# Cross-attention on one core: the low weights' last 64 rows as row halves beside the scores, for V as for K

## What is computed

```python
h = _layernorm(x, gamma, beta)                       # x: 8 x 256 x 256
Q = (h @ Wq).reshape(B, NQ, N_HEADS, HEAD_DIM)       # Wq: 256 x 1024
K = (context @ Wk).reshape(B, NC, N_HEADS, HEAD_DIM) # context: 8 x 256 x 192
V = (context @ Wv).reshape(B, NC, N_HEADS, HEAD_DIM)
attn = jnp.einsum('bihd,bjhd->bhij', Q, K)
attn = jax.nn.softmax(attn, axis=-1) * scale
vals = jnp.einsum('bhij,bjhd->bihd', attn, V).reshape(B, NQ, INNER)
out = x + vals @ Wo + bo
```

## Time and profile before

| What | Value |
|---|---|
| median of three runs | 364.79 us |
| the profiled execution, time of its run | 364.5 us |
| its span, first to last instruction | 362.6 us |
| what lies around the span | 1.9 us |
| granted TensorE clock over the span | 0.999 of full speed |
| busy: PE, DVE, ACT, POOL | 97%, 67%, 70%, 45% |
| share of the chain that ended last: PE | 92% |

### The profile page before, as it was taken

How to read it: one execution, slowest core, us unless ns; L and a number is a source line. 1 busy time by engine, 2 the same in 40 slices (tenths; PEclk the granted TensorE clock), 3 DMA queues, 4 the chain that set the end, 5 groups by cost and what they waited for, 6 DMA issues and landing times.

```text
span 362.6 us, 8915 instructions
## 1 busy us (share of the span) xinstructions
PE 353.0 (97%) x3116; PEld 305.8 (84%) x3116; DVE 242.9 (67%) x534; ACT 252.1 (70%) x762; POOL 164.5 (45%) x321
## 2 busy tenths in 40 slices
PE   5999999999999999999999999999999999999986
PEld 5779888888888888988888988888988888988865
DVE  5887566866568666686667675686565866566654
ACT  4898876766677766777766776766677766677762
POOL 5677884335444262444532464323744325344321
PEclk9999999999999999999999999999999999999999
DMA  6930010200002000020000100020000000000000
GB/s 191 272 118 3 1 52 2 82 0 3 2 0 82 0 0 0 0 80 0 1 0 29 51 0 0 0 78 1 0 0 0 29 2 0 2 2 31 3 0 31
DMA packets 10743, 10.39 MB, mean 29 GB/s; under 512 B 960, under 2 KB 10176, under 8 KB 10720
## 3 DMA queue, kind: packets, MB, share of 16 engines
q1 hardware_dynamic: 10192, 9.64, 8.6%
q10 hardware_dynamic: 416, 0.33, 0.3%
q0 software_dynamic: 112, 0.13, 0.2%
HBM read 8.00 MB, written 2.10 MB: 28 GB/s over the span
## 4 chain that ended last, share of the span: by engine, by line
PE 92%; ACT 3%; DVE 3%; DMA 1%; issue 0%; POOL 0%; DVEq 0%
PE mix_ps L710 16%; PE st_ps L805 15%; PE st_ps L688 13%; PE o_ps L777 12%; PE w_ps L752 12%; PE w_ps L730 12%; PE w_ps L823 10%; ACT prob L405 2%; DMA x_in<-in_x_dram 1%; PE w_ps L671 1%; PE w_ps L663 1%; ACT qk_hi L415 0%; DVE w_lo L480 0%; DVE neg_max L563 0%; DVE qk_lo L576 0%
## 5 line engine op out<-in xcount | busy, mean ns | idle before, releaser
L316 POOL TENSOR_SCALAR prob<-prob,inv 128x256 f32<-128x256 f32 x256 | 120.1, 485 | 158.0 <-DVE inv L570 157.6
L405 ACT ACTIVATE prob<-st_ps,neg_max 128x256 f32<-128x256 f32 x256 | 118.0, 473 | 27.0 <-DVE neg_max L563 27.0
L563 DVE TENSOR_REDUCE neg_max<-st_ps 128x2 f32<-128x512 f32 x128 | 82.5, 683 | 35.2 <-PE st_ps L688 34.9
L458 ACT ACTIVATE prob_t<-st_ps 128x512 f32<-128x512 f32 x64 | 38.4, 600 | 44.2 <-PE st_ps L805 44.2
L638 DVE COPY prob_t<-st_ps 128x512 f32<-128x512 f32 x64 | 44.1, 691 | 28.6 <-PE st_ps L805 25.2
L710 PE MATMUL mix_ps<-prob_t,v_sb 128*64 128x256 f32 x504 | 61.5, 385 | 0.1
L805 PE MATMUL st_ps<-ident,prob 128*128 128x128 f32 x512 | 61.1, 272 | 0.0
L805 PEld LDWEIGHTS st_ps<-ident,prob 128*128 128x128 f32 x512 | 56.7, 141 | 0.1
L576 DVE TENSOR_TENSOR qk_lo<-w_ps,qk_hi 128x512 fp32r<-128x512 f32 x62 | 42.8, 690 | 20.6 <-ACT qk_hi L415 20.6
L405 ACT ACTIVATION_READ_ACCUMULATOR prob<-st_ps,neg_max 128x1 f32 x256 | 52.7, 206 | 0.0
L710 PEld LDWEIGHTS mix_ps<-prob_t,v_sb 128*64 128x64 f32 x504 | 33.4, 136 | 17.9 <-issue 0.3
(11 more groups left out here) (121 smaller groups left out, 589.1 us busy)
## 6 DMA issues: line engine op xcount, KB each, us to landing
x_in<-in_x_dram SPq DMA_DIRECT2D x8, 256.0 KB, 3.1
out_dram<-y_sb SPq DMA_DIRECT2D x7, 256.0 KB, 2.2
c_in<-in_ctx_dram SPq DMA_DIRECT2D x7, 192.0 KB, 2.9
w_raw<-in_L_xattn_Wq_dram SPq DMA_DIRECT2D x8, 128.0 KB, 3.3
w_raw<-in_L_xattn_Wo_dram SPq DMA_DIRECT2D x4, 256.0 KB, 3.5
w_raw<-in_L_xattn_Wk_dram SPq DMA_DIRECT2D x4, 128.0 KB, 4.0
w_raw<-in_L_xattn_Wk_dram SPq DMA_DIRECT2D x8, 64.0 KB, 3.6
w_raw<-in_L_xattn_Wv_dram SPq DMA_DIRECT2D x2, 256.0 KB, 3.5
```

The costliest lines, as they stand in the source:

```text
L316: last = nc.gpsimd.tensor_scalar(prob[:, e, r, :], prob[:, e, r, :], inv[:, e, r:r + 1], SCALE, ALU.mult, ALU.mult)
L405: last = nc.scalar.activation(prob[:, e, r, :], st_ps[e][:, r * ROWS:(r + 1) * ROWS], ACT.Exp, bias=neg_max[:, e, r:r + 1], accum_out=sums ...
L458: nc.scalar.activation(prob_t[:, e, :, :].rearrange("p a b -> p (a b)"), st_ps[e][:, :], ACT.Copy)\
L563: nc.vector.tensor_reduce(neg_max[:, e, :], st_ps[e][:, :].rearrange("p (r j) -> p r j", r=RT), AX, ALU.max, negate=True).then_inc(max_rea ...
```

## The change

- **K.** For steps 1 to 30, each pair's product with the last low rows is left out of `keys`. A new `keys_rest(u)`, between `scores(u)` and `mix(u - 1)`, does both pairs at once: the first pair on rows 0 to 63 of the array and the second on rows 64 to 127, 64 rows each, the high part of the context alone. It opens the banks `w0_ps` and `w1_ps`, and so waits for `v_ready`.
- **V.** From the third V on, the 512 columns are halved over `w0_ps` and `w1_ps`: four products of 256 columns for each half at the end of a step, and the last low rows as two 64-row products (`values_rest`) at the start of the next step, ahead of the scores. ACT copies V out in two pieces.
- **A second copy** of the high part's last 64 rows, `c_rest`, on partitions 0 to 63: one more ACT piece in `context_hi`.
- **Order of the turns.** As V's second half takes `w1_ps`, `turn_c` and `turn_x` stand between `output(u - 1)` and `turn(u)`, each behind a wait for both `qk_lo` of the step. `context_hi` and `context_lo` move into the context step, ahead of the copies of `prob_t`; `norm` moves to the end of the context step, behind these copies; `hidden` moves into the x step; `statistics` move one step ahead. V's second half waits for `context_lo` or for the first half of `hidden` where such a turn was made.
- **PE's program** has no loop any more.

```diff
+    V_HALF = GROUP * P // 2
+        c_rest = sb("c_rest", [HALF, 2, ROWS], fp32r)
-        LOAD, STATS, TURN_C, NORM, SPLIT_C, SPLIT_H, PUT = -5, -4, -4, -3, -3, -2, PER_SEQ + 1
+        LOAD, STATS, TURN_C, TURN_X, SPLIT_H, PUT = -5, -5, -4, -3, -2, PER_SEQ + 1
...
             def context_hi(b, ps):
                 nc.scalar.activation(c_t[:, b % 2, 0, :], ps[:, 0:ROWS], ACT.Copy)
+                nc.scalar.activation(c_rest[:, b % 2, :], ps[HALF:P, ROWS:2 * ROWS], ACT.Copy)
...
                 if 2 <= u < STEPS:
-                    values_out(u, w0_ps)
+                    act.wait_ge(v_made, u + 1 + turns(8))
+                    for k, ps in enumerate((w0_ps, w1_ps)):
+                        last = nc.scalar.activation(
+                            v_sb[:, u // RT % 2, u % RT, k * V_HALF:(k + 1) * V_HALF],
+                            ps[:, 0:V_HALF], ACT.Copy)
+                    last.then_inc(v_ready, 1)
...
+                b = of_seq(u, TURN_C, 2)
+                if b is not None:
+                    act.wait_ge(c_turned, b + 1 + turns(2))
+                    context_hi(b, context_bank(b))
+                b = of_seq(u, TURN_X, 1)
+                if b is not None:
+                    act.wait_ge(h_lo_ready, DT * b + turns(4))
+                    act.wait_ge(x_turned, b + 1 + turns(2))
+                    hidden(b, w1_ps)
...
+            def keys_rest(u):
+                b, p = divmod(BATCH * (u + 1), PAIRS)
+                pe.wait_ge(v_ready, RT if u == 1 else u + 1)
+                pe.wait_ge(qk_lo_ready, BATCH * (u + 1))
...
+                high = (c_rest[:, b % 2, :], c_t[HALF:P, b % 2, 1, :])
+                for a in range(BATCH):
+                    own = slice(a * HALF, (a + 1) * HALF)
+                    nc.tensor.matmul(qk_banks(u)[a][:, 0:ROWS],
+                                     w_lo[own, K0 + 1, (p + a) * P:(p + a + 1) * P], high[a],
+                                     start=True, stop=False, skip_group_check=True)
...
+                for a in range(2):
+                    pe.wait_ge(qk_lo_ready, BATCH * n + a + 1)
+                    seq = of_seq(n - 1, TURN_C, 2)
+                    if a == 1 and seq is not None:
+                        pe.wait_ge(c_lo_ready, seq + 1)
+                    seq = of_seq(n - 1, TURN_X, 1)
+                    if a == 1 and seq is not None:
+                        pe.wait_ge(h_full_ready, DT * seq + 1)
+                    first = half * PIECE + a * V_HALF
+                    for m, (w, i, k) in enumerate(passes[:-1]):
...
+                        nc.tensor.matmul((w0_ps, w1_ps)[a][:, 0:V_HALF], c_t[:, b % 2, k, rows],
+                                         w[:, i, first:first + V_HALF],
+                                         start=m == 0, stop=False, skip_group_check=True)
+            def values_rest(n):
...
+                high = (c_rest[:, b % 2, rows], c_t[HALF:P, b % 2, 1, rows])
+                for a in range(2):
+                    own = slice(a * HALF, (a + 1) * HALF)
+                    first = half * PIECE + a * V_HALF
+                    last = nc.tensor.matmul((w0_ps, w1_ps)[a][:, 0:V_HALF], high[a],
+                                            w_lo[own, V0 + 1, first:first + V_HALF],
+                                            start=False, stop=True, skip_group_check=True)
+                last.then_inc(v_made, 1)
...
+            def step(u):
+                if 2 <= u < STEPS:
+                    values_rest(u)
                 if 0 <= u < STEPS:
-                    scores(u, turns)
+                    scores(u)
+                if 1 <= u < STEPS - 1:
+                    keys_rest(u)
...
+                b = of_seq(u, TURN_C, 2)
+                if b is not None:
+                    pe.wait_ge(c_loaded[b % 2], 16 * (b // 2 + 1))
+                    pe.wait_ge(qk_lo_ready, BATCH * u + HEADS)
+                    turn_c(b, context_bank(b))
+                b = of_seq(u, TURN_X, 1)
+                if b is not None:
+                    pe.wait_ge(x_norm_ready, b + 1)
+                    pe.wait_ge(qk_lo_ready, BATCH * u + HEADS)
+                    turn_x((w1_ps, w1_ps), ROWS)
                 if 0 <= u < STEPS:
-                    turn(u, turns)
+                    turn(u)
                 if 1 <= u < STEPS - 1:
-                    values(u + 1, turns)
...
-            walk(pe, step, 2)
+            for u in range(-1, LAST):
+                step(u)
```

More of the change, by code:

```diff
@@ L308, in step @@
                     weight_lo(14)
-                b = of_seq(u, NORM, 1)
+                b = 1 if u == 1 else of_seq(u, TURN_C, 2)
                 if b is not None:
@@ L388, in step @@
                 if 2 <= u < STEPS:
-                    values_out(u, w0_ps)
[L390 to L399, removed]
+                    act.wait_ge(v_made, u + 1 + turns(8))
[4 more added lines that the diff above has]
+                    last.then_inc(v_ready, 1)
+                if u == 1:
+                    act.wait_ge(c_turned, 2)
+                    context_hi(1, context_bank(1))
                 def probabilities(e):
@@ L583, in step @@
                 maximum(1)
-                b = of_seq(u, SPLIT_C, 1)
-                if b is not None:
-                    context_lo(b, context_bank(b), turns)
+                if u == 1:
+                    context_lo(1, context_bank(1), turns)
                 maximum(2)
@@ L627, in step @@
                     weight_lo(16)
-                if b is not None and b >= 2:
-                    dve.wait_ge(x_turned, b + turns(2))
-                    norm(b, turns)
+                b = of_seq(u, TURN_C, 2)
+                if b is not None:
+                    context_lo(b, context_bank(b), turns)
                 if 0 <= u < STEPS:
@@ L641, in step @@
                             weight_lo(13)
+                b = of_seq(u, TURN_C, 2)
+                if b is not None:
+                    dve.wait_ge(x_turned, b + turns(2))
+                    norm(b, turns)
                 b = of_seq(u, STATS, 2)
@@ L716, in mix, with keys @@
                         last.then_inc(mixed, 1)
-            def keys(t, a, turns, parts=(0, 1)):
+            def keys(t, a, parts=(0, 1)):
                 b, p = divmod(t, PAIRS)
@@ L756, in queries, with output @@
                 last.then_inc(projected, 1)
-            def output(w, turns):
+            def output(w):
                 b, s = divmod(w, PER_SEQ)
@@ L798, in last_output, with turn @@
                             last.then_inc(o_added, 1)
-            def turn(u, turns):
+            def turn(u):
                 for e in range(HEADS):
-                    pe.wait_ge(scaled, HEADS * u + e + 1 + turns(32))
+                    pe.wait_ge(scaled, HEADS * u + e + 1)
                     for r in range(RT):
@@ new lines, in values_rest @@
+            def values_rest(n):
+                g, j = divmod(n, RT)
+                b, half = divmod(g, 2)
+                rows = slice(j * P, (j + 1) * P)
+                high = (c_rest[:, b % 2, rows], c_t[HALF:P, b % 2, 1, rows])
[5 more added lines that the diff above has]
+                                            start=False, stop=True, skip_group_check=True)
@@ L836, in _ @@
             for a in range(BATCH):
-                keys(a, a, lambda n: 0)
+                keys(a, a)
             for a in range(BATCH):
-                queries(a, a, lambda n: 0)
+                queries(a, a)
             for a in range(BATCH):
-                keys(BATCH + a, a, lambda n: 0, parts=(0,))
-            def step(u, turns):
+                keys(BATCH + a, a, parts=(0,))
+            def step(u):
+                if 2 <= u < STEPS:
+                    values_rest(u)
                 if 0 <= u < STEPS:
-                    scores(u, turns)
+                    scores(u)
+                if 1 <= u < STEPS - 1:
+                    keys_rest(u)
                 if 1 <= u <= STEPS:
-                    mix(u - 1, turns)
+                    mix(u - 1)
                 for a in range(BATCH):
@@ L850, in step @@
                     if 0 <= u and t < BATCH * STEPS:
[L851 to L866, removed]
+                        keys(t, a, parts=(1,) if u == 0 else (0, 1))
+                        queries(t, a)
                 if 1 <= u < STEPS:
-                    output(u - 1, turns)
+                    output(u - 1)
                 if u == STEPS:
```

89 lines of the change are left out of this document (49 added, 40 removed).

## The result

The changed kernel takes **370.79 us** (median of five runs, 370.58 to 371.05), the kernel before 364.80 us beside it. The ratio is 1.0166, with a 95% interval from 1.0152 to 1.0180: 1.7% slower, 6.0 us. Forecast were 370.9 us, slower with a chance of 0.86.

The account below looks back on a forecast made before the run. PE was taken as the bound in every step. Saving -5.7, start +0.4, context steps +4.0, x steps +6.6 and step 1 +0.8 sum to +6.1 on 364.5, so 370.6; the median 0.3 above, 370.9 us; range 365.4 to 373.0.

Parts of the forecast that it names:

- The saving: PE, steps 1 to 30: K 0.12 and V 0.07 less, together 0.19 a step, -5.7 us.
- the third rival: The halves don't run side by side: two pairs a step cost 0.12 more each, +7.2, 378.1 us; chance 0.03.
- the first rival: Faster, the waits don't show: saving stays, only the start's 0.4 is paid, -5.3, 359.5 us; chance 0.07.
- The start: Before the first scores: a third piece in `context_hi` delays PE, bounds 0 and 0.4, taken as +0.4 us.
- The wait ahead of the turns: PE between `output` and the turn waits for `qk_lo`: 0.31 plus 0.16 restart, 0.47 us lost.
- the restart: PE going on after a wait costs more, read from step 31: 0.05 + 0.11 = 0.16 us.
- V's second half, and the late maximum: Context step: PE loses 0.19 waiting at V's second half; DVE starts the x step's maximum 0.78 us late.
- The x steps: ACT catches up 0.15 of 0.78, so PE waits 1.10 ahead of `turn_x`; six steps, +6.6 us.
- Step 1: `norm` stands ahead of its second `qk_lo`: a wait between 0.47 and 1.10, taken as +0.8 us.
- The three waits: PE's waits in six context steps (+4.0), six x steps (+6.6) and step 1 (+0.8 us).
- Nothing carries over: All 13 turns from step 1 cost 0.47, but x steps' DVE and V's second half aren't late: 365.6 us; chance 0.12.
- The program's packets: PE's written-out program needs some 13 more instruction packets; rival if PE waits for each: +12, 382.9 us; chance 0.02.

Follow-up runs that it names:

- the kernel with the low part behind the copies: Changed kernel with the turned context and x put in `mix_ps`, and `context_lo` placed after DVE's two copies of `prob_t`: 359.43 us, ratio 0.9854 to the kernel before.
- The edit of `norm`: Against the changed kernel, `norm` of the third and later sequences goes back into the x step, between the second inverse and `mix_lo`: 367.66 us.

## Why the prediction was right

**The saving.** Forecast were 0.12 for K and 0.07 for V in a step; undone one at a time, plain steps grow by 0.12 (K, in the changed kernel) and 0.07 (V, in the kernel with the low part behind the copies). The halves do run side by side. K's pair in a plain step of the changed kernel:

```profile
224.64 0.28 PE L766 MATMUL w_ps<-c_rest,w_lo 64*128 64x256 f32 x1
224.65 0.28 PE L766 MATMUL w_ps<-c_t,w_lo 64*128 64x256 f32 x1
```

That settles the third rival. With the waits taken away, the kernel comes to the first rival's time: 359.43 against 359.5. Its condition, `qk_lo` before `output`, did not hold; a bank that needs no `qk_lo` does the same.

**The start.** +0.4 forecast. The first keys wait for the context's low part until 8.32, 7.95 in the earlier trace rows, and the first scores start at 12.65 instead of 12.26: +0.39.

```profile
8.32 0.42 PEld L748 LDWEIGHTS w_ps<-c_t,w_hi 128*128 128x128 f32 x3 [0.64 <-DVE c_t L523]
```

**The wait ahead of the turns.** 0.47 forecast, 0.47 measured in the context step. It comes apart as worked out: `qk_lo` ends at 196.32 + 0.69 = 197.01, and `output` would have gone on at 196.57 + 0.12 = 196.69, so 0.32 (forecast 0.31); PE starts 0.15 after `qk_lo` (forecast 0.16 for the restart). The restart's size was right, but not how it falls: the prediction read it from step 31 as 0.05 ahead of the first product and 0.11 behind it.

**V's second half, and the late maximum.** Here two terms were off, and they offset each other. The low part ends at 199.46 + 0.43 = 199.89, 2.27 after the turn's start (forecast 2.26), and PE goes on at 200.03, 0.19 lost as forecast. But the products behind the restart run slower too, another 0.07, which the step left out. That makes the context step 11.64 instead of the 11.5 forecast. It also moves the next scores back, so that the maximum, 202.49 - 197.62 = 4.87 after the turn (forecast 4.90), is 0.69 late and not 0.78.

By the sentence of the Trainium skill that the prediction draws on (VectorE: DVE Perf Modes, section The DRAIN you can't avoid) that start would have been 0.21 later. The same paragraph goes on that a next operation that is not held starts earlier. The rows fit that: 0.74 for the two pieces of `norm`, and 1.88 for three maxima where a single one takes 0.69.

**The x steps.** The mis-sized term: 1.10 forecast, 0.96 measured. From the lateness of 0.69, `qk_lo` keeps 0.50 (its end is 209.14 - 201.06 = 8.08 after the scores, 230.96 - 223.38 = 7.58 in the plain step), so ACT and DVE caught up 0.19 instead of 0.15. 0.47 + 0.50 gives the 0.96 within rounding. The edit of `norm` tested this: the 0.50 went and the 0.47 stayed.

**Step 1.** This term was too small. Forecast were +0.8 of waiting, which with the 0.19 saved is +0.6; the step grew by 0.88 (11.96 to 12.84). `output` to `turn_x` takes 0.96 more there. `norm`, ahead of the second `qk_lo`, makes the wait as long as in an x step; the value taken was the middle of its bounds, and the upper end (1.10) was nearer. A second wait stood behind this one: in the kernel with the low part behind the copies, where no `qk_lo` is asked for, 0.28 stays, as the turn then waits for `norm` itself:

```profile
30.66 0.42 PEld L682 LDWEIGHTS mix_ps<-ident,x_norm 128*128 128x128 f32 x4 [0.32 <-DVE x_norm L514]
```

**The sum.** Forecast +6.1, measured +6.2 in the span: the start 0.39, step 1 0.88, the six context steps 6 x 0.57 = 3.4, the x steps 6 x 0.80 = 4.8, and some -3.3 from the others. The forecast had 2.8 and 5.5 for the two kinds and 0.6 for step 1, so its total is better than its parts: too little for context steps and step 1, too much for x steps, and that these cancel is luck. The three waits were put at 4.0 + 6.6 + 0.8 = 11.4; the kernel with the low part behind the copies is 370.79 - 359.43 = 11.36 faster than the change. By its steps that is 6 x 0.77 = 4.6, 6 x 0.99 = 5.9 and 0.65, so this match too is closer than its parts.

**The rivals.** "Nothing carries over" (365.6) fell with the first maximum, 0.69 late. The program's packets came as guessed, 26 instead of the 13 of the earlier trace rows:

```profile
q8 instruction: 26, 0.43, 0.5%
```

The steps that they belong to take 10.44 to 10.45, and no wait names them.

Advanced Engine Details and Errata of the Trainium skill, section ISA Cache, gives TensorE 128 KB in lines of 16 KB. The trace agrees on the lines, 26 packets with 0.43 MB. The section names no price for a line that has to be fetched, so the prediction's remark that trace and page differ on the cost reads more into the page than it says; no run here shows PE waiting for one.

One reading of the code was loose: the count that V's second half waits for in an x step stands for both pieces of `hidden`, not for the first. That wait cost nothing, since V's second half follows there without a gap.

## What to carry to other kernels

Two products that run side by side in place of two full ones save little per step, and the price is paid where their buffers come from: with the turns moved ahead, into a bank that DVE was still reading, a low part (`qk_lo`) that nobody had needed early became a wait of the engine that bounds. Before giving a buffer away, list what was kept in it, what its next writer would then wait for, and look for a bank that the bounding engine's own order has already freed. And where a covered wait leaves the step as long as it was, look for a second one behind it.

## What was not expected

- In these steps a restart of PE costs about 0.15 from the release to the first product (0.05 in step 31), and then 0.02 (ahead of the transposes, 0.46 instead of 0.44) to 0.07 (ahead of V's products) more in those behind it.
- In the kernel with the low part behind the copies, a first maximum 1.81 after the scores' first product, 0.9 later than in a plain step, lengthened no step.
